# Engine orders written anew: the same instructions of six interleaved streams in another sequence on each engine

## The reference, cut to what matters

```python
xn = _layernorm(x)
x = x + _L0_attn_ref(xn, ...) + _L0_ffn_ref(xn, ...)
xn = _layernorm(x)
x = x + _L1_attn_ref(xn, ...) + _L1_ffn_ref(xn, ...)
```

## Time and profile before

| | before |
|---|---|
| median of 3 runs | 2267.91 us (2267.54 to 2269.87) |
| the profiled execution | 2270.01 us |
| its span, first to last instruction | 2268.0 us |
| mean granted TensorE clock | 0.91 |
| PE busy | 1957.7 us (86%) |
| DVE, ACT, POOL busy | 62%, 42%, 36% |

### The profile page before, as it was taken

One profiled execution on the slowest core, in us unless ns is written; L12 is line 12 of the kernel. 1 busy time (PEld: TensorE's weight loads), 2 busy tenths in 40 slices (PEclk: granted clock), 3 DMA queues, 4 the chain that ended last, 5 costly groups with the idle time before them and its releaser, 6 DMA issues. The chain is left out here.

```text
span 2268.0 us, 40783 instructions
## 1 busy us (share of the span) xinstructions
PE 1957.7 (86%) x15104; PEld 1291.3 (57%) x15104; DVE 1401.9 (62%) x3394; ACT 947.8 (42%) x2465; POOL 824.7 (36%) x823
## 2 busy tenths in 40 slices
PE   3797779998899988998899988998799988998686
PEld 1594448564685557654585557654585556754332
DVE  3553465775758756775757756775767847674442
ACT  1413442365424652265424643265514653264023
POOL 4506550444406541443506542353505442160000
PEclk9788898999899998999899998999999998999557
DMA  4200012100311012200302012100212012100200
GB/s 167 50 20 15 17 35 62 53 14 15 77 36 41 18 40 61 53 14 15 78 24 54 18 38 64 53 14 11 71 31 57 14 31 74 47 16 1 75 1 6
DMA packets 124820, 89.71 MB, mean 40 GB/s; under 512 B 42168, under 2 KB 111928, under 8 KB 124344
## 3 DMA queue, kind: packets, MB, share of 16 engines
q1 hardware_dynamic: 124016, 85.39, 14.0%
q0 software_dynamic: 320, 1.05, 0.1%
q10 hardware_dynamic: 288, 0.67, 0.1%
HBM read 46.84 MB, written 25.17 MB: 32 GB/s over the span
## 5 line engine op out<-in xcount | busy, mean ns | idle before, releaser
L1636 POOL TENSOR_TENSOR soft<-soft,prec 128x512 f32<-128x512 f32 x128 | 135.7, 1066 | 541.6 <-DVE prec L1295 540.5
L1163 ACT ACTIVATE shared<-bank 128x512 f32<-128x512 f32 (+1 forms) x384 | 202.7, 528 | 254.3 <-PE bank L931 252.3
L1447 DVE TENSOR_REDUCE nmx<-bank 128x1 f32<-128x512 f32 (+3 forms) x352 | 224.6, 638 | 105.3 <-PE bank L909 104.4
L1083 ACT ACTIVATE soft<-bank,nmax 128x128 f32<-128x128 f32 x512 | 180.2, 384 | 169.4 <-DVE nmax L1287 168.7
L1597 POOL TENSOR_TENSOR qk_rs<-qk_rs,minus_half 128x16 f32<-128x16 f32 x64 | 187.8, 2935 | 5.3
L930 PE MATMUL bank<-b_sb 128*128 128x128 bf16 x512 | 118.0, 231 | 41.6 <-ACT shared L1163 39.7
L931 PE MATMUL bank<-shared 75*128 75x384 bf16 (+3 forms) x512 | 149.5, 318 | 0.0
L621 PE MATMUL bank<-w_sb,hT 128*128 128x512 f32 x256 | 136.7, 620 | 8.7 <-DVE hT L1237 5.7
L909 PE MATMUL bank<-shared 72*128 72x256 bf16 (+3 forms) x512 | 135.9, 317 | 0.0
L1595 POOL TENSOR_SCALAR rs_f<-mv_f 128x4 f32<-128x4 f32 x24 | 5.6, 234 | 344.2 <-DVE mv_f L1226 344.2
L593 PE MATMUL bank<-c_sb,soft 128*128 128x128 f32 x608 | 106.3, 308 | 27.5 <-POOL soft L1636 22.4
(11 more groups left out here) (236 smaller groups left out, 4809.1 us busy)
## 6 DMA issues: line engine op xcount, KB each, us to landing
shared<-parts_dram SPq DMA_DIRECT2D x64, 288.0 KB
vm<-v_f SPq DMA_DIRECT2D x112, 128.0 KB, 2.3
parts_dram<-parts SPq DMA_DIRECT2D x96, 128.0 KB, 2.5
L_dram<-shared SPq DMA_DIRECT2D x32, 256.0 KB, 2.5
shared<-X_dram SPq DMA_DIRECT2D x32, 256.0 KB, 3.0
shared<-L_dram SPq DMA_DIRECT2D x32, 256.0 KB, 3.8
w_sb<-weights SPq DMA_DIRECT2D x1, 4167.0 KB, 21.2
x_tm<-x SPq DMA_DIRECT2D x8, 256.0 KB, 3.1
```

The costliest lines, as they stand in the source:

```text
L1083: a = af(v4(p_sb, 2, 4)[:, j, g], place("fS", j)[:, g * P:(g + 1) * P], ACT.Exp, bias=nmax[:, at:at + 1], accum_out=psums[:, at:at + 1])
L1163: af(v4(PTm, 2, GROUP)[:, u % 2, i, 0:n], place("mST")[:, 0:n], ACT.Exp).then_inc(mexp_done, 1)
L1447: reduce(v3(nmx[:], HM)[:, h:h + len(heads), c], v3(place("mS")[:, 0:len(heads) * (c + 1) * P], len(heads)), AX, ALU.max, negate=True).the ...
L1636: tt(p, p, spread(prec[:, at:at + NPAIR], P), ALU.mult).then_inc(fnorm_done, 1)
```

## The change

Only the five strings in `ORDER` differ. Each has the same letters in the same numbers, so each engine issues the same instructions; only the shuffle of the streams is another one.

```diff
 ORDER = {
     "PE": (
-        "ddbddfdfddmmddfddmdddbbddbfbffbdddfmfdbbmbfmbfffbmmbdbmbdddbdddddddddbdddmdmdddbdbdddbdddddddddddbdddbdmdddbdb"
-        "dbbbbbdmabamfafamdfamfafamfamafaffabafmfaamacbcfacmacbacacbacmacbacfacacbcafcfamacbcbaccbacfcabcafcacfacbcafcf"
-        "amabccacfcabcmcabcacbcabcafcfamabccabcmcabcfabccafcbcfcmcccfcbccfbccbbbbbfcbccbccccccbccc"),
+        "ddbddfddfddmfmddfdmbdddbddbffbfdbdddffmbmbbfbffbmmdbbddddddddddddbdddbdbdddmdbdbddbdbddbddddbdbbdbbbbddbdddfdf"
+        "ddfdfdfdmdffffbaffamadamaabbabamabaffafabafmacfaccbacbacacbacfacacbacacfcfacbacfacfcacmfacfacbcbaccbacbacmacba"
+        "cacfacmfacbacmacbaccbacbfacmcabccafcafcamcaccabcfcmcbcbbbbbmccbcmcbcmcccmcbcmccmcccmccmcc"),
     "ACT": (
-        "dddddbddffddddmdmbbbffffdbddfdbbbfffffmmbmbmdbmbdddddddbddbdbdddddddddbdmddbddffmdffffmffffbcbccmcbcbcffccfccb"
-        "cfcbcbfcbcfccfcfccbcmbfcfcccbcbcccbcfbfcbcmcbcfccfccfccfcccfbcfccccccccbc"),
+        "ddddddfbddfdddmbdmbffbfffddbddbbffbfffbmmdmbbdddddddbddbmdbdbddddddddbbfdfdffdfdmdffffbdfbbfbmfffbfcccbcbcfcbc"
+        "fccfcfccfcbcfcfcbcbcbccmccbcfcbcfcbcbcfccmcfcfcccccfcbcmccccccmccccccmcbc"),
     "DVE": (
-        "ddbdddbmddbfdmfmmddmbmddbfbmbfmdddbmbmbbmmmmddbdddddddddbdddbmbmdddddddddddddddddbbdddbmdbdddbbbbmadbamafamfam"
-        "afamafamaafabamabfabmaamaaamabaaabababmafacafabaaafbabafabmafamacababababmafafamabbabfbcmfbbbbbbbcc"),
+        "ddbddddfbmddbfmmmddmdbdfbfbmbmdddbmbmbbmmddddddddddddddbbddbdbmmddddbbddbddbddbddbbbddbdddffddddffmdfabamababa"
+        "famaaabamaabafabbfamaaaaaaabfaafabafcabbmafafaaabamabaabmabaamcafabbafabamabamaabmbbbcmbmbmbmmmmcmc"),
     "POOL": (
-        "dddddbbfffmffbbfffffbbbbbdfffffffffffbfbfffbbffffffbbbbfffffbfffffb"),
+        "ddddbdbfffffmfbbffffbbbbbffffffdfbbfffffffffbbfffffbbfffffbbffbfffb"),
     "SP": (
-        "mddfdddfddmddaffafaffafafc"),
+        "mddfdddfddmddfaffaffaaffac"),
 }
```

## The result

The changed kernel takes 2191.04 us (median of 4 runs, 2186.19 to 2197.5) against 2268.89 us (2267.54 to 2270.38) of the kernel before beside it: ratio 0.9659, 95% interval 0.9629 to 0.9688. The forecast was 2212, in a range of 2155 to 2270; the narrower range, 2190 to 2240, held by 1 us. The profiled execution is one of the longer ones, 2197.5 us with a span of 2195.4; it is 72.5 us under that of before, where the prediction had 55.5.

A forecast was written before the change was run, and what follows sets the result against it. PE was taken as the busiest engine, so only its idle time and half-clock products could be won: -38.5 us for periods 1 to 7, -11 for period 0, -6 for period 8, together -55.5, giving 2212 us, range 2155 to 2270.

The forecast's parts named there:

- Ahead of the inverse: Stretch around `solve`, periods 1 to 7: `solve` and `fS` 2 come 2.2 us earlier, the rest even; -2.2 us a period.
- Feed-forward into the inverse: Layer 0's feed-forward and layer 1's first `fqk` move into the inverse and sequence, which have no idle time: 0 us.
- The start of the scores: Where layer 1's scores begin: PE waits about 6 us for POOL's 26.5 us run, against 5.2 idle now; +0.8 a period.
- The last group: Period's end, seven expert products fill c's last group: -2 idle there, -1 idle in front, -1.7 by the clock; -4.7 a period.
- The halving: Last group of values: of 3.4 us hanging on the clock only half, 1.7 us a period, was counted.
- Period 0: First period, three streams: feed-forward moved into the inverse and sequence -9.4, earlier `solve` -2.2, POOL +0.6; -11 us.
- Period 8: Last period: first `mS` 5 us earlier, experts among `mST` +8, groups before -9; -6 us.
- +8: Last 39 us of period 8: eight new expert products among `mST`, at half clock hiding less than half of themselves, cost 8 us.
- -9: Period 8, groups before the last 39 us: they lose about as many experts, saving 9 us.
- The rule on the shared port: Around `solve`: POOL products beside DVE ones cost their length, up to 1.4 us a period, giving 2222 us; not in the sum.
- B: Rival for the whole order: waits only move, periods 1 to 7 win nothing; 2268 us, chance 0.08.
- C: Rival: fill works everywhere, clock stays up; -11.5 a period, period 0 -14, period 8 -10; 2164 us, chance 0.22.

The follow-up runs named there:

- e9: Kernel before, with the new order only for each period's first steps, up to `fS` 2 and the second `mq`, `gate` still ahead of the inverse: 2273.96 us, ratio 1.0022.
- e10: Changed kernel with two more roots of 128x16 on POOL ahead of `delta_norm` in each of the 8 batches: 2266.89 us, ratio 0.9999.
- e11: Kernel before, order untouched, with 20 small unread products at the waits of the last group of values in periods 1 to 7: 2243.2 us, ratio 0.9889.
- e1: Changed kernel with the orders of before in periods -1, 0 and 8: 2220.51 us, ratio 0.9791.
- e2: Changed kernel with the orders of before in period 8 alone: 2203.65 us, ratio 0.9718.
- e5: Kernel before, with the experts alone moved to their places in the new order, the gate left in the old one: 2381.71 us, ratio 1.0494.
- e6: Changed kernel, with gate and experts taken back to their places in the order of before: 2406.74 us, ratio 1.0609.
- e12: Changed kernel with unread products at waits in periods 0 and 8, and only ahead of `fS` 2 in the periods between: 2166.56 us, ratio 0.9556.

## Why the prediction was right, and where it was wrong

Direction and range held, and the 38.5 us for periods 1 to 7 came out as 40.6 (41.6 by the mean of four executions). But that sum was right by terms that weren't, so its closeness is luck; over the whole program the gain was 78 us where 56 were forecast. Of the signs named, the earlier `solve`, the wait ahead of `fS` 2, `gate`, POOL without a gap and the first `mS` came; the waits for POOL, the idle time at a period's end and the lengths of periods 0 and 8 did not.

- *Ahead of the inverse, -2.2.* `solve` began 1.7 us earlier, of which 0.9 is the clock of the first `k`; PE's wait ahead of `fS` 2 fell by 0.65 (4.30 to 3.65). `gate` costs 1.0 in place of a wait of 0.7 and 1.9 of work, as said. The earlier `solve` by itself wins nothing (e9). Over-sized.
- *Feed-forward into the inverse, 0.* The work did fit in, but the stretch took up to 6.8 us of half clock with no idle time in it. The same `inv_zx` took 1.79 us where it stands beside other streams' products, and 1.84 to 1.91 before; such tenths are the likely source of the 1.4 us a period in the row "rest". That is argued, not shown.
- *The start of the scores, +0.8.* This step failed. I let PE wait 6 us for POOL; it waits 0.5 a period, and the waits for POOL over seven periods became 3.5 us. Since other short waits came, idle time in the stretch as a whole went from 5.2 to 4.5 us only, -0.7 where the term had +0.8. POOL does run nearly without a gap there, as predicted (905 to 950 in period 3, with gaps of 0.6 and 0.5), but it comes just in time. e10 shows that it is just: 6.6 us more and all of it is waited for.
- *The last group, -4.7.* Idle time fell by 0.7, not by 2: the waits ahead of `aT` (0.87) and the last `mPV` (0.47) went, but `mST` kept its four (2.1 us in all, 2.2 before), `final` kept 0.78, and a new one of 0.72 stands ahead of `matg`. In period 3 the clock gave all of its 3.4 and the first `k` of the next period 0.9 more. The halving, "as the stretch is still not dense", was the wrong choice: it was at 1.00 with 3.6 us idle in 17.1. e11 puts the clock at 3.3 in the mean, the first `k` included.
- *Period 0, -11.* Measured -16.9, and -18.5 by the means. Idle time gave 7.5, and the clock 9.1: the 17 us at half clock in the first sequence (132.4 to 149.4 above), which e1 and e11 have there too, don't occur in the new order. No term spoke of it.
- *Period 8, -6.* Measured -15.9, -9 by the means and -13 by e2. The first `mS` came 6 us earlier (5 predicted). Two steps failed, in opposite directions. One is "+8" for eight experts among `mST` "at half clock": the stretch went to full clock, the experts took 0.9 to 1.0 us each, and the part came out 5.9 us shorter, 6.2 by the means. The other is "-9" for the groups before, which lost 4 us in this pair of profiles, and by the means are 3 us longer (95.7 to 99.1).
- *The rule on the shared port.* `solve` takes 11.1 to 11.2 us after and 10.8 before, in seven periods of each. Two of its products are lengthened beside a scaling of POOL in either order, 1.08 and 0.79 us before, 0.98 and 0.81 after; those after are longer ones. By the Trainium skill ("SBUF — State Buffer", section "SBUF: two separate sides") I had named up to 1.4 more (the sum took none of it); this trace has 0.3 to 0.4.

Of the rivals, B is out as to the time, though a part of the waits did only move, as it said (15.3 us of idle time gone where waits for POOL lost 31). C came nearest in its mechanism, the clock, and let too much idle time go. Its sum was also wrong: the terms that it names, with the forecast's for the rest, make -14.2 a period and not -11.5, hence some 2145 us instead of 2164. That 2164 is close to what the order gives together with unread products (2167) is chance.

What stays open: what sets off the half clock in stretches without idle time, and which of the moves in the middle carries the gain. e5 and e6 only show that the experts and the rest can't be had one without the other. Nor was the old order run with unread products in all its waits, as e12 has them in the new one; so how much of the new order's gain such products alone would bring is known only for the ends of periods 1 to 7 (24 of 76 us).

## What to carry to other kernels

Read a stretch by three numbers, idle time, time lost to half clock, and the rest; an edit that fills gaps was paid here by the second about as much as by the first, and the price of a wait is the wait plus the half-clock stretch behind it. Read more than one execution before a share is given to the clock. Before orders are rewritten, try unread products in the waits: at the ends of periods 1 to 7 they took 24 us off the old order, and in periods 0 and 8 and behind `solve` 24 off the new one. Fixed orders on five engines interlock, so cost a moved step on every engine that has a part of it (gate and expert 0 moved back cost 8.9 us a period), and don't expect half of a new order to give half of its gain.

## What the runs showed of the hardware that I had not expected

PE can be busy without a gap and still at 1.2 GHz: 17.00 us of 17.00 busy at a clock of 0.50 in period 0 before, and 13.70 of 13.70 in e5. (The profile models where products end, so gaps too short for it aren't excluded.) And the same instructions in the same order vary in it: period 8 took 155.0, 161.8 and 157.6 us in the new order, and 164.2 to 171.0 in the old one. That fits the spread of the runs, 11.3 us over the 4 of the changed kernel and 11.1 over the 19 of before that were taken beside the last experiments. The 2.8 us over the 4 runs of before in the result above were too few to show it.
